# Q, K and V of an attention layer parked in DRAM in another layout and another order

## What is computed

```python
def _L1_attn_ref(x, Wq, bq, Wk, bk, Wv, bv, Wo, bo):
    HIDDEN = 512
    NUM_HEADS = 32
    HEAD_DIM = HIDDEN // NUM_HEADS      # 16
    THRESH = 0.001
    q = (x @ Wq.T + bq).reshape(B, S, H, D)
    k = (x @ Wk.T + bk).reshape(B, S, H, D)
    v = (x @ Wv.T + bv).reshape(B, S, H, D)
    scores = jnp.einsum('bshd,bsgd->bshg', q, k) * inv_sqrt_d
    scores = jnp.where(scores > THRESH, scores, -jnp.inf)
    attn = jax.nn.softmax(scores, axis=-1)
    out = jnp.einsum('bshg,bsgd->bshd', attn, v).reshape(B, S, Hd)
    return out @ Wo.T + bo
```

## Time and profile before

| | |
|---|---|
| median of three runs | 2693.41 us (2692.19 to 2694.73) |
| profiled execution | 2690.72 us, its span 2689.1 us |
| mean granted clock of TensorE | 0.866 of full speed |
| busy share of the span: TensorE, VectorE, ScalarE, GpSimd | 75%, 62%, 42%, 46% |
| DMA | 159.22 MB, mean 59 GB/s |

### The profile page before, as it was taken

One profiled execution on the slowest core, in us unless ns is written; L12 is line 12 of the kernel. 1 busy time (PEld: TensorE's weight loads), 2 busy tenths in 40 slices (PEclk: granted clock), 3 DMA queues, 4 the chain that ended last, 5 costly groups with the idle time before them and its releaser, 6 DMA issues. The chain is left out here.

```text
span 2689.1 us, 38861 instructions
## 1 busy us (share of the span) xinstructions
PE 2008.5 (75%) x13952; PEld 1672.7 (62%) x13952; DVE 1672.9 (62%) x3825; ACT 1127.7 (42%) x2538; POOL 1241.8 (46%) x966
## 2 busy tenths in 40 slices
PE   6599999999999537332438999999999994281334
PEld 1478888888888436331436888888888873261324
DVE  1667666667666785453646666666667677745345
ACT  1355555555555314232124555555555551251311
POOL 0454554555555345344235454554554543363532
PEclk9799999999999868755668999999999997595566
DMA  5300100100101012766031000100100100148641
GB/s 217 102 17 24 40 16 24 40 17 24 40 16 34 26 59 78 181 127 161 16 111 40 24 17 24 40 17 24 40 17 24 40 17 28 51 160 162 110 123 39
DMA packets 164217, 159.22 MB, mean 59 GB/s; under 512 B 73764, under 2 KB 123940, under 8 KB 161460
## 3 DMA queue, kind: packets, MB, share of 16 engines
q1 hardware_dynamic: 149652, 136.91, 18.4%
q10 hardware_dynamic: 14368, 19.78, 2.2%
HBM read 123.07 MB, written 33.59 MB: 58 GB/s over the span
## 5 line engine op out<-in xcount | busy, mean ns | idle before, releaser
L970 POOL TENSOR_TENSOR gqa_rot<-gqa_rot,consts 128x512 f32<-128x512 f32 x160 | 207.0, 1294 | 631.1 <-ACT gqa_rot L786 631.0
L802 ACT ACTIVATE gqa_prob<-gqa_prob,gqa_nmax 128x128 f32<-128x128 f32 (+3 forms) x512 | 282.0, 552 | 186.8 <-DVE gqa_nmax L890 186.7
L890 DVE CUSTOM_DVE_ANT_0 gqa_prob<-gqa_pS,consts 128x128 f32<-128x128 f32 (+3 forms) x512 | 219.9, 486 | 68.8 <-PE gqa_pS L686 68.8
L898 DVE TENSOR_TENSOR gqa_ptl<-gqa_pT,gqa_pth 128x384 fp32r<-128x384 f32 (+1 forms) x384 | 217.9, 595 | 51.7 <-ACT gqa_pth L812 51.7
L430 PE MATMUL ln_pT<-consts,ln_xn 128*128 128x128 f32 x256 | 58.2, 420 | 252.2 <-DVE ln_xn L409 252.2
L973 POOL TENSOR_TENSOR gqa_full<-gqa_full,gqa_rot 128x512 f32<-128x512 f32 x160 | 207.2, 1295 | 39.0 <-DVE gqa_full L861 28.7
L812 ACT CAST gqa_pth<-gqa_pT 128x384 fp32r<-128x384 f32 (+1 forms) x384 | 185.8, 518 | 92.7 <-PE gqa_pT L701 89.6
L740 PE MATMUL gqa_pW<-woh,gqa_oh 128*128 128x512 f32 x504 | 211.9, 421 | 1.7 <-DVE first_y L915 1.7
L430 PEld LDWEIGHTS ln_pT<-consts,ln_xn 128*128 128x128 f32 x256 | 51.6, 225 | 259.1 <-DVE ln_xn L409 259.0
L907 DVE TENSOR_SCALAR gqa_prob<-gqa_prob,gqa_rden 128x128 f32<-128x128 f32 (+3 forms) x512 | 208.8, 471 | 4.6
L982 POOL TENSOR_TENSOR gqa_ql<-gqa_full,gqa_qh 128x512 fp32r<-128x512 f32 x128 | 165.4, 1292 | 73.9 <-DVE gqa_qh L879 73.9
(11 more groups left out here) (227 smaller groups left out, 5578.6 us busy)
## 6 DMA issues: line engine op xcount, KB each, us to landing
raw_q<-in_wq SPq DMA_DIRECT2D x16, 1024.0 KB, 5.5
raw_o<-in_wo SPq DMA_DIRECT2D x16, 1024.0 KB, 5.3
mod_wm<-in_wmod SPq DMA_DIRECT2D x8, 1536.0 KB, 19.4
raw_kv<-in_wkv SPq DMA_DIRECT2D x16, 512.0 KB, 6.7
kp<-qkv_part SPq DMA_DIRECT2D x32, 256.0 KB, 2.5
heads_kk<-kp SPq DMA_DIRECT2D x8, 1024.0 KB, 8.8
attn<-heads_o SPq DMA_DIRECT2D x16, 512.0 KB, 8.2
wo_at<-attn SPq DMA_DIRECT2D x32, 256.0 KB, 7.2
```

What stands on the lines that cost most here:

```text
L802: ins = nc.scalar.activation(p, p, ACT.Exp, scale=-1.0, bias=nmax[r][:, i:i + 1], accum_out=den[r][:, i:i + 1])
L890: nc.vector.tensor_tensor_reduce(prob[r][:, P_OFF[i]:P_OFF[i] + w], pS[s][:, c:c + w], held.mask[:, T - w:T], -1.0, LARGEST, ALU.add, ALU.min,
L898: nc.vector.tensor_tensor(ptl[:, c:c + w], pT[k % 2][:, 0:w], pth[:, c:c + w].bitcast(F32), ALU.subtract).then_inc(pt_lo, 1)
L970: nc.gpsimd.tensor_tensor(rot[r % 2][:], rot[r % 2][:], held.sinT, ALU.mult).then_inc(sined, 1)
```

## The change

Three things. The order of the items becomes V, K, Q. V is stored head by head (vp has the shape (2, 4, 32, 32, 4, 48): token block, head, l, block, numbers), by four transfers for each item in runs of 96 bytes, and read back in runs of 6 KB into a bd of another order of dimensions without padding; the last of the four groups of products (i = 1) then works on 16 instead of 32 columns for each block. And kp and qp have l outermost, (2, 32, parts, 16, 512), so that a store writes 1 KB runs that lie a whole (parts x 16 x 512) apart, by four transfers for K and three for Q, one for each part, and a load reads a partition's 16 KB as 16 runs of 1 KB.

```diff
--- before.py
+++ after.py
@@ -227,7 +227,7 @@
         pass
 
 
-QKV_ORDER = (1, 0, 2)
+QKV_ORDER = (2, 1, 0)
 
 
 class QkvWeights:
@@ -1075,10 +1075,10 @@
         stored = [st.sem(f"stored{i}") for i in range(NB)]
         items = [(w, b, m) for w in QKV_ORDER for b in range(HB) for m in range(KT)]
         N = len(items)
-        FIRST_V = 2 * HB * KT
+        NV = HB * KT
         total, stored_by = [0] * NB, []
         for n, (w, b, m) in enumerate(items):
-            total[n % NB] += 32 if w == 1 else 16
+            total[n % NB] += (48, 64, 64)[w]
             stored_by.append(total[n % NB])
 
         def slot(n, s):
@@ -1100,15 +1100,13 @@
                     sp.wait_ge(third, n + 1)
                     src = part[n % NB]
                     if w == 2:
-                        sp.dma_start(a["vp"][b].rearrange("(t r) x -> r t x", r=KT)[m], src[:]).then_inc(stored[n % NB], 16)
+                        for j in range(4):
+                            sp.dma_start(a["vp"][b, j, :, :, m].rearrange("g l x -> l g x"),
+                                         src[j * LO:(j + 1) * LO].rearrange("p (g x) -> p g x", g=H1)).then_inc(stored[n % NB], 16)
                         continue
-                    src = src[:].rearrange("p (s x) -> p s x", s=3)
-                    dst = a["kp" if w == 1 else "qp"][b, :, 4 * m:4 * m + 4].rearrange("s d l x -> (d l) s x")
-                    if w == 0:
-                        sp.dma_start(dst, src).then_inc(stored[n % NB], 16)
-                    else:
-                        sp.dma_start(dst[:, 0:2], src[:, 0:2]).then_inc(stored[n % NB], 16)
-                        sp.dma_start(dst[:, 2:4], src[:, 0:3:2]).then_inc(stored[n % NB], 16)
+                    dst = a["kp" if w == 1 else "qp"][b, :, :, 4 * m:4 * m + 4].rearrange("l s d x -> s d l x")
+                    for to, part_no in enumerate((0, 1, 0, 2) if w == 1 else (0, 1, 2)):
+                        sp.dma_start(dst[to], src[:, part_no * T:(part_no + 1) * T]).then_inc(stored[n % NB], 16)
                 for i in range(NB):
                     sp.wait_ge(stored[i], total[i])
 
@@ -1116,10 +1114,10 @@
             def _(pe):
                 for n, (w, b, m) in enumerate(items):
                     if n >= 6:
-                        if n - 6 < FIRST_V:
-                            pe.wait_ge(left, n - 5)
+                        if n - 6 < NV:
+                            pe.wait_ge(turned, n - 5)
                         else:
-                            pe.wait_ge(turned, n - 5)
+                            pe.wait_ge(left, n - 5 - NV)
                     for k in range(KT):
                         if b == 0 and m == 0 and n:
                             pe.wait_ge(w_lo, (QKV_ORDER.index(w) - 1) * KT + k + 1)
@@ -1157,7 +1155,7 @@
 
                 act.wait_ge(b_scaled, 1)
                 for n in range(N + 2):
-                    if n < FIRST_V:
+                    if NV <= n < N:
                         leave(n)
                     if 1 <= n < N + 1:
                         firsts(n - 1)
@@ -1171,8 +1169,8 @@
                     if n < N:
                         if n >= NB:
                             dve.wait_ge(third, n - NB + 1)
-                        if n < FIRST_V:
-                            dve.wait_ge(left, n + 1)
+                        if n >= NV:
+                            dve.wait_ge(left, n - NV + 1)
                             nc.vector.transpose(rest[n % NB][:], flat[n % NB][:]).then_inc(turned, 1)
                         else:
                             dve.wait_ge(full, n + 1)
@@ -1216,7 +1214,7 @@
         NR, NS, NO = 4, 5, 3
         qq = [st.sb(f"qq{i}", [P, LU, T], BF16) for i in range(2)]
         kk = [st.sb(f"kk{i}", [P, LU, T], BF16) for i in range(2)]
-        bd = [st.sb(f"bd{i}", [P, 4 * LU, 4, 64], BF16) for i in range(2)]
+        bd = [st.sb(f"bd{i}", [P, 4, 4 * LU, VW], BF16) for i in range(2)]
         prob = [st.sb(f"prob{i}", [P, TC, H1]) for i in range(NR)]
         pt = [st.sb(f"pt{i}", [P, TC, H1]) for i in range(NR)]
         pp = [st.sb(f"pp{i}", [P, 3, TC, H1], BF16) for i in range(NR)]
@@ -1237,7 +1235,7 @@
         def load_scores(eng, u):
 
             b, ls = u // 2, slice(u % 2 * LU, u % 2 * LU + LU)
-            lanes = lambda name, s0, s1: a[name][b, s0:s1, :, ls, :].rearrange("s d l x -> (s d) l x")
+            lanes = lambda name, s0, s1: a[name][b, ls, s0:s1].rearrange("l s d x -> (s d) l x")
             for lo, s0, s1 in ((0, 0, 2), (2, 0, 4)):
                 eng.dma_start(kk[u % 2][lo * D1:(lo + s1 - s0) * D1], lanes("kp", s0, s1)).then_inc(qk_in[u], 16)
             for lo, s0, s1 in ((0, 0, 3), (3, 0, 2), (5, 0, 1)):
@@ -1247,9 +1245,8 @@
 
             b, l0 = u // 2, u % 2 * LU
             for j in range(4):
-                t0 = (LO * j + l0) * KT
-                src = a["vp"][b, t0:t0 + KT * LU, :].rearrange("t (g x) -> g t x", g=H1)
-                eng.dma_start(bd[u % 2][32 * j:32 * j + 32, :, j, 0:VW], src).then_inc(v_in[u], 16)
+                src = a["vp"][b, j, :, l0:l0 + LU].rearrange("g l r x -> g (l r) x")
+                eng.dma_start(bd[u % 2][32 * j:32 * j + 32, j], src).then_inc(v_in[u], 16)
 
         with nc.Block() as block:
 
@@ -1300,9 +1297,10 @@
                     for l in range(LC):
                         for n, (i, m) in enumerate(((0, 0), (0, 1), (0, 2), (1, 0))):
                             for r in range(4):
-                                mm = pe.matmul(pO[c % NO][32 * r:32 * r + 32, l, :].rearrange("p (j x) -> p j x", j=4),
+                                x = slice(0, 2 * D1) if i == 0 else slice(0, D1)
+                                mm = pe.matmul(pO[c % NO][32 * r:32 * r + 32, l, :].rearrange("p (j x) -> p j x", j=4)[:, :, x],
                                                pp[c % NR][:, m, 4 * l + r, :],
-                                               bd[u % 2][:, s0 + 4 * l + r, :, 32 * i:32 * i + 32], start=(n == 0), stop=(n == 3))
+                                               bd[u % 2][:, :, s0 + 4 * l + r, 2 * D1 * i:2 * D1 * i + x.stop], start=(n == 0), stop=(n == 3))
                     mm.then_inc(o_full, 1)
 
                 LAG = 6
@@ -1659,7 +1657,7 @@
     a["out"] = nc.dram_tensor("out", (B * T, D), F32, kind="ExternalOutput").ap()
     a["gates"] = nc.dram_tensor("gates", (4, B, D), F32).ap()
     a["row_scale"] = nc.dram_tensor("row_scale", (D,), F32).ap()
-    for n, shape in (("qp", (HB, 3, D1, LO, T)), ("kp", (HB, 4, D1, LO, T)), ("vp", (HB, T, H1 * VW))):
+    for n, shape in (("qp", (HB, LO, 3, D1, T)), ("kp", (HB, LO, 4, D1, T)), ("vp", (HB, 4, H1, LO, KT, VW))):
         a[n] = nc.dram_tensor(n, shape, BF16).ap()
     a["attn"] = nc.dram_tensor("attn", (HB, 2, D, T), F32).ap()
     build(nc, a)
```

## The result

The changed kernel takes 2783.39 us (median of four runs, 2778.18 to 2784.34), the kernel before 2692.8 us beside it; the ratio is 1.0335, 95% interval 1.0318 to 1.0351. The profiled execution of the changed kernel has a span of 2782.7 us, 93.6 us over the one of before. 2781 us were forecast.

The account below looks back on a forecast made before the run. TensorE was taken to bound stage_qkv, the four units' loads stage_head_attention; after the change, stores would bound K and Q. Twice (52 - 8) = +88 us on the 2689.1 us span gave 2781 us; range 2735 to 2925.

Parts of the forecast that it names:

- K and Q stores on four engines: stage_qkv: outermost count 4 leaves 4 of 16 engines, 47.5 ns a run, 85.1 us; sign: quarter share, 70 to 90 GB/s.
- rival 1: K and Q stores: engines stay in step on one partition group, 85 ns a run, +67 us a half, 2915; chance 0.17.
- V's stores: stage_qkv: 96-byte runs at 12.3 ns each, 3.15 us an item, the last store ending at 1071.6.
- Rival 2: V's stores pay 46.5 ns a run like the attn stores, +61 us a half, 2903; chance 0.12.
- The sum for stage_qkv: K and Q stores queue behind V's, so the next stage starts at 1159.0 instead of 1106.7: +52 us.
- The loads: stage_head_attention: V loads faster, SP no longer blocked in them, K and Q slightly slower: about -8 us a half.
- the +0.5 us for a unit from 1 KB runs: K and Q loads: reading 1 KB runs adds 0.5 us a unit, four times a half.
- V's gain: V loads take 4.1 us a unit instead of 6.3; unit 3's scores start at 1190.2 instead of 1200.94.
- V's issues: stage_head_attention: V loads issued on SP in 1 to 2 us, where SP sat 11.99 us in one before.
- The groups of partitions: K and Q loads: SBUF side limits each partition group to about 24 GB/s; unit 0's five landings were said to agree.
- rival 3: K and Q stores use 16 engines anyway, so the layout doesn't cost: 2687; chance 0.08.
- Rival 4: DRAM distance limits K and Q loads, 24 us a half faster: 2639 with 16 engines (0.05), 2733 with four (0.06).

Follow-up runs that it names:

- e2_two_d: Changed kernel with each K and Q store cut in two, so that 2 head dimensions instead of 4 lie outermost: 2932.32 us (one run).
- e3_v_only: Changed kernel with K's and Q's layout taken back, keeping the order V, K, Q and V's new layout: 2675.06 us, 0.9952 of before.
- e8_kq_only: Changed kernel with V's layout, bd and products taken back, keeping K's and Q's new layout and the order: 2786.66 us, 1.0353 of before.
- e5_pad: e1_by_d with two unused 1 KB rows behind each l in kp and qp: 2715.49 us (one run).
- e1_by_d: Changed kernel with K and Q stores cut by head dimension instead of by part, 32 partitions a transfer: 2728.73 us, 1.0158 of before.

## Why the prediction was right

- **K and Q stores on four engines.** Shown: share 0.27, 91 and 96 GB/s, and 16, 4 and 2 engines in three kernels, by rates and by small packets. (The sign was 70 to 90 GB/s, so both rates lie just above it.) Size: 45.0 ns a run for K and 42.7 for Q instead of 47.5, so 4.19 MB in 46.1 us and 3.15 MB in 32.8 us, 78.9 us for the 85.1 of the forecast.
- **In step on one group (rival 1).** Not seen. Two engines whose partitions share groups, in e2_two_d, keep 42.7 ns a run, not 85.
- **V's stores.** 101 GB/s over seven items is 27 us, 15.2 ns a run, where 12.3 were taken from the load; the end is at 1076 instead of 1071.6. Rival 2, at 46.5 ns, is out. e3_v_only shows that little of this term is left if K and Q are not behind it at a quarter of the engines: stage_qkv grows by 2.1 us instead of the 4 to 5 that I had put for 16 engines.
- **The sum for stage_qkv.** 1156.90 for 1159.0: the store runs were dearer by 6 us for K and Q in the forecast, cheaper by 4 for V. The stage itself is +48 us a half for +52, as it also starts 1.2 us later than before in this half and grows by 2 us less in the second.
- **The loads.** This is the term that was mis-sized: -8 us a half were forecast, -2.4 measured, and unit 3's scores start 91.4 us after the first load, not 86. Two sizes in it failed. The first is the +0.5 us for a unit from 1 KB runs. The layout of K and Q costs the heads stage 4.6 us (the changed kernel over e3_v_only) to 5.7 us a half (e8_kq_only over before), not 2, and unit 0 alone 2 to 3 us. I had taken K's 64 partitions at 360 GB/s as a sign that 1 KB runs would not matter. e5_pad shows that where they lie does (1.5 us of unit 0's 2.3); what their length costs isn't separated. The second is V's gain: 1200.94 - 1190.2 is 10.7 us, measured were 7.0 (e3_v_only). The place is V of unit 2, which waits for unit 0's products: it was forecast 62 us after the first load, and is issued at 65.6 in e3_v_only, 69.0 in the changed kernel, 69.2 before. I had let TensorE follow its loads at once. In e3_v_only it doesn't wait for unit 2's loads at all, but has its own gaps of 7 us, which stood in no row that I read. That these gaps are the missing 3.7 us is likely, but not shown.
- **V's issues.** The sign was 1 to 2 us. Unit 0's V took 2.81 us, unit 1's 4.04, unit 2's 1.76. SP's blocking moved to the Q loads, 15.04 and 17.58 us.
- **The groups of partitions.** The prediction lets all five landings of unit 0 agree with 24 GB/s for each group. The last one does so only with a condition: 16 partitions in 1.4 us are 187 GB/s, as much as the 32 before them got, where half the groups should give half, unless the two ran side by side. No row settles it.
- **Rivals 3 and 4.** e1_by_d is rival 3 with SP's issues added, and lands at +36 to +42 us, so the term for issues, hidden behind the slow stores in the changed kernel, would have been the largest there (15 of the 23 us a half that stage_qkv grew). Rival 4, faster loads, has the wrong sign: the loads became slower.
- **The total.** 2 x (48 - 2.4) = 91 us for the 88 forecast: the stores came out 4 us a half cheaper, the loads 5.6 us dearer, and these two misses nearly cancel. That the total came out within 3 us of 2781 is luck; the mechanism of the large term is not.

## What to carry to other kernels

Before a DRAM layout is changed, write down for each transfer what its outermost dimension counts on both sides after the change: here a 128 became a 4, twelve of sixteen DMA engines fell silent, and stores that had always been hidden became the longest thing in their stage. Undo a change in parts even when the sum is understood: V's half of this one was worth 0.5% by itself. And where the cut of a transfer can be chosen, count SP's time for each issue too, 0.44 to 0.64 us here.

## What was not expected of the hardware

- The DMA engine's pace for 1 KB writes hardly depends on how many work: 42.7 ns a run on two, 42.7 (Q) and 45.0 (K) on four, 47.5 on sixteen.
- 96-byte writes to DRAM at 384-byte steps run at 15.2 ns each for an engine (101 GB/s in all), a quarter above the 12.3 ns of such reads, in a stream of 27 us.
- Two unused rows of 1 KB after each 48 or 64 made stage_qkv of e1_by_d 6 us a half shorter and its unit 0 loads 1.5 us (one run of e5_pad, both halves); on four engines the stores gained 1 us a half.
- A gap of 7 us in TensorE's own instruction stream, for which the profile names no releaser, goes to 2 us when the DMA engines are idle, and is 2.4 us when V's layout alone is put back.
